# Language-model tower, one core: GpSimd and ScalarE reordered round the low parts of u and xT

## The reference

```python
h = weight[x] * keep_mask[x]                       # 32 x 512 x 256
n = (h - mean(h)) / sqrt(var(h) + 1e-5)
u, res = split(n @ in_proj_w.T, [512])             # 512 columns of u, 256 of res
u = causal_conv4(u, conv_w) + conv_b               # four taps for each channel
delta = softplus(u @ dt_proj_w.T + dt_proj_b)
g = u * sigmoid(delta)
y = scan(state = 0.9 * state + 0.1 * g)            # along the tokens
h = h + y @ out_proj_w.T + res
n2 = layernorm(h)
xd, wd = mx_quantise(n2), mx_quantise(ffn_weight)  # fp6 values, one scale for 32 columns
h = h + xd @ wd.T + ffn_bias
```

## Time and profile before

| quantity | value |
|---|---|
| median of 3 runs | 1024.26 us (1023.52 to 1025.87) |
| the profiled execution | 1026.02 us, of which the trace spans 1024.2 us |
| mean granted clock of TensorE | 0.988 |
| busy: PE, DVE, POOL, ACT | 93%, 81%, 73%, 63% of the span |

### The profile page before, as it was taken

One profiled execution on the slowest core, in us unless ns is written; L12 is line 12 of the kernel. 1 busy time (PEld: TensorE's weight loads), 2 busy tenths in 40 slices (PEclk: granted clock), 3 DMA queues, 4 the chain that ended last, 5 costly groups with the idle time before them and its releaser, 6 DMA issues.

```text
span 1024.2 us, 14964 instructions
## 1 busy us (share of the span) xinstructions
PE 955.7 (93%) x4892; PEld 781.8 (76%) x4892; DVE 829.8 (81%) x1218; ACT 647.2 (63%) x1342; POOL 750.3 (73%) x749
## 2 busy tenths in 40 slices
PE   2689999999999999999999999999999999999996
PEld 1476887777877778787777788777878787878885
DVE  4767988888888888898888888888889878889866
ACT  5755666666667766666676666766666666665541
POOL 6647777777787777878777788777787787776652
PEclk9889999999999999999999999999999999999998
DMA  5213432244433234443223443323444322343101
GB/s 170 69 35 103 123 91 81 88 115 124 124 103 95 77 93 123 123 123 102 77 88 103 123 123 108 94 76 91 123 123 123 102 68 88 112 124 103 62 23 42
DMA packets 73790, 100.81 MB, mean 98 GB/s; under 512 B 12577, under 2 KB 61089, under 8 KB 73761
## 3 DMA queue, kind: packets, MB, share of 16 engines
q1 hardware_dynamic: 67616, 83.59, 25.7%
q0 software_dynamic: 6144, 16.85, 7.2%
HBM read 51.65 MB, written 48.76 MB: 98 GB/s over the span
## 4 chain that ended last, share of the span: by engine, by line
POOL 41%; issue 21%; DVE 20%; PE 9%; ACT 7%; DMA 1%; POOLq 0%; DVEq 0%; ACTq 0%
POOL g_lo L381 16%; POOL rows L366 11%; DVE u L757 10%; POOL xT_lo L430 5%; ACT n L558 4%; DVE h L767 3%; DVE stats L773 3%; POOL rstd L415 3%; POOL h L425 3%; ACT u L515 2%; PE psZ L1074 1%; PE psZ L1068 1%; PE psZ L1067 1%; POOL nmr L419 1%; POOL u_lo L388 1%
## 5 line engine op out<-in xcount | busy, mean ns | idle before, releaser
L757 DVE SCALAR_TENSOR_TENSOR u<-psU,cw,u 128x511 f32<-128x511 f32 x378 | 260.0, 741 | 82.6 <-ACT u L515 80.2
L388 POOL TENSOR_TENSOR u_lo<-u,u_hi 128x512 fp32r<-128x512 f32 x128 | 164.5, 1296 | 83.1 <-ACT u_hi L522 79.0
L1074 PE MATMUL psZ<-u_lo,dt_hi 128*128 128x512 f32 x512 | 208.9, 408 | 12.5 <-POOL u_lo L388 12.5
L381 POOL TENSOR_TENSOR g_lo<-g,g_hi 128x512 fp32r<-128x512 f32 x128 | 199.8, 1580 | 20.6 <-ACT g_hi L533 19.9
L1067 PE MATMUL psZ<-u_hi,dt_hi 128*128 128x512 f32 x512 | 201.4, 393 | 5.7 <-ACT u_hi L522 4.6
L1068 PE MATMUL psZ<-u_hi,dt_lo 128*128 128x512 f32 x512 | 202.2, 395 | 0.0
L522 ACT ACTIVATE u_hi<-u 128x512 fp32r<-128x512 f32 x128 | 81.0, 633 | 138.4 <-DVE u L757 137.7
L366 POOL DMA_INDIRECT rows<-table,ids x128 | 127.1, 993 | 44.9 <-issue 44.1
L1074 PEld LDWEIGHTS psZ<-u_lo,dt_hi 128*128 128x128 f32 x512 | 96.5, 188 | 58.9 <-POOL u_lo L388 40.7
L515 ACT ACTIVATE u<-psU,cb,cw 128x512 f32<-128x512 f32 x126 | 94.3, 772 | 39.7 <-PE psU L1010 39.6
L533 ACT ACTIVATE g_hi<-g 128x512 fp32r<-128x512 f32 x128 | 76.6, 621 | 62.3 <-DVE g L837 62.3
(11 more groups left out here) (120 smaller groups left out, 2215.5 us busy)
## 6 DMA issues: line engine op xcount, KB each, us to landing
turned_n<-nb_blocks SPq DMA_DIRECT2D x31, 512.0 KB
nT<-turned_n SPq DMA_DIRECT2D x124, 128.0 KB
out<-h SPq DMA_DIRECT2D x31, 512.0 KB, 4.6
turned<-xb SPq DMA_DIRECT2D x30, 512.0 KB, 2.6
xT<-turned SPq DMA_DIRECT2D x120, 128.0 KB, 2.9
rows<-table,ids POOLq DMA_INDIRECT x128
dt_stage<-dt_wT SPq DMA_DIRECT2D x1, 1024.0 KB, 5.8
g<-in_wT SPq DMA_DIRECT2D x1, 768.0 KB
```

Of the source, the lines that this page charges most:

```text
L381: pool.tensor_tensor(g_lo[:, m, :], g[:, m, :], f32(g_hi[:, m, :]), ALU.subtract).then_inc(g_lo_ready[m], 1)
L388: pool.tensor_tensor(u_lo[:, m, :], u[:, m, :], f32(u_hi[:, m, :]), ALU.subtract).then_inc(u_lo_ready[m], 1)
L757: dve.scalar_tensor_tensor(u[:, m, back:T], u_psum_tile(st, m)[:, 0:T - back], cw[:, m, TAPS - 1 - back:TAPS - back], u[:, m, back:T], ALU ...
L1074: ins = pe.matmul(psZ[:, m % 2, :], dt_hi[:, k, o], u_lo[:, k, :], start=False, stop=(k == M - 1))
```

## The change

On POOL, g_lo(3) goes ahead of add_bias, mean1 goes behind u_lo(0) and u_lo(1), xT_lo goes ahead of u_lo(2) and u_lo(3), and variance1 with inverse_root1 goes behind them. On ACT, xT_hi goes ahead of the first taps of u(2) and u(3), and the four squares go behind u_hi(2) and u_hi(3). No instruction is added, taken out or changed in size.

```diff
@@ POOL @@
+                if st.back:
+                    split_g(M - 1, s - 1)
                 if st.tail:
                     add_bias()
-                if st.back:
-                    split_g(M - 1, s - 1)
...
-                if st.early:
-                    mean1(2)
                 split_u(0)
                 split_u(1)
                 if st.early:
+                    mean1(2)
+                if st.tail:
+                    split_xT()
+                split_u(2)
+                split_u(3)
+                if st.early:
                     variance1(2)
                     inverse_root1(2)
-                split_u(2)
-                split_u(3)
-                if st.tail:
-                    split_xT()
@@ ACT @@
                 if st.early:
                     mask_rows(2)
-                    square1_rows(2)
+                if st.tail:
+                    split_xT()
                 if not st.first:
                     first_tap(2)
                     first_tap(3)
-                if st.tail:
-                    split_xT()
                 split_u(2)
                 split_u(3)
+                if st.early:
+                    square1_rows(2)
                 if st.early:
                     normalise1(2)
```

## The result

The changed kernel takes **1080.86 us** (median of 3 runs, 1080.83 to 1081.92) against 1024.26 before: a ratio of 1.0553, with a 95% interval of 1.0529 to 1.0577. That is 56.6 us slower. The forecast was slower by 28.2 us, 1053, with a range up to 1069. The direction was right, the size was half of what was measured, and the time lies outside the range.

The account below looks back on a forecast made before the run. PE was taken as the pace until the delayed layer-norm chain replaced it. 0.78 + 0.72 - 0.38 = 1.12 us a step over 27 steps, plus 0.8, less 2.8, gave +28.2: 1053 us, range 1034 to 1069.

Parts of the forecast that it names:

- slack of 0.95 us behind turn_n1: DVE's only slack behind turn_n1, ahead of add_linear; it absorbs 0.95 us of the delay, the rest lengthens the period.
- PE sets the pace: In a full step PE, busy 93% of the span, bounds the kernel; its gaps are at most 2.1 us a step.
- Part 1: POOL's low parts for PE come earlier; alone this would give PE 1.4 us a step back (bounds 1.2 and 2.1).
- each becomes ready before PE asks: g_lo(3), u_lo(0), u_lo(1) and xT_lo, moved earlier on POOL, would no longer keep PE waiting.
- Part 2: ACT's first taps of u(2) and u(3) start 1.60 us earlier; waiting for xT's loads taken as 0, at most 0.3.
- Part 3: Squares and root behind u_hi(3) delay normalise1: turn_n1 1.73 us late, add_linear 0.78 us late, the period longer by 0.78.
- Part 4: POOL's first two g_lo meet DVE's quantisation: round_to_grid's end loses 0.72 us a step, dequantise gives back 0.38.
- rival (b): A worse collision: scale issued over about 1.25 us after the g_lo pair starts; 1.8 us a step, 1071 us; 13%.
- The ends: Steps 30 and 31 have no first layer norm, so PE keeps its prize there: 2.8 us back in all.

Follow-up runs that it names:

- e12: The kernel before plus one tiny POOL operation and a wait for it between the gathers and g_lo(0): 1032.58 us.
- e11: The kernel of e5 plus a tiny POOL operation and a wait for it between the gathers and g_lo(0): 981.05 us.
- e1: The changed kernel, with POOL waiting for DVE's round_to_grid ahead of g_lo(0) in every step from 1 on: 1055.37 us.
- e5: The changed kernel with ACT's squares back behind the first taps, ahead of u_hi(2), and POOL's root ahead of u_lo(2): 1018.29 us.
- e9: The changed kernel plus one tiny POOL operation and a wait for it between the gathers and g_lo(0): 1069.57 us.
- e2: The changed kernel, with POOL waiting ahead of g_lo(0) only until DVE's scale is done: 1068.83 us.
- e8: The changed kernel, with POOL waiting for the end of its own g_lo(0) ahead of g_lo(1): 1065.97 us.
- e10: The kernel of e7 plus a tiny POOL operation and a wait for it between the gathers and g_lo(0): 1060.49 us.
- e7: The kernel before with only the squares moved behind u_hi(3), and epsilon and root behind u_lo(3): 1163.31 us.
- e6: The order of e5, with POOL also waiting for DVE's round_to_grid ahead of g_lo(0): 984.23 us.

## Why the prediction was right and wrong

**What bounds the kernel: right on the slack, too simple on the pace.** The slack of 0.95 us behind turn_n1 decided, as said. But "PE sets the pace" was read from PE's busy share. The chain of the same page gave PE 9% and POOL 41%, and in e12 0.27 us more on DVE came with 0.3 more in the period. This did not make the forecast miss, since the cost was rightly counted from DVE's gapless stretch.

**Part 1: the size right, one statement not.** With the squares out of the way (e11) the period is 28.5 to 28.9 us, so the moves together are worth 1.3 to 1.7 us a step; 1.4 was taken. In e11 PE's loads wait 13.6 us for u_lo instead of 34.0, and the linear layer's wait for xT_lo has left the list. But "each becomes ready before PE asks" did not hold for u_lo in the changed kernel: PE's loads wait 35.6 us for it. There it costs nothing that the rows show, as PE is not in the circle.

**Part 2: right.** The second taps start 1.60 us earlier, as forecast. xT's loads landed in time: ACT never waited for that DMA in the changed kernel's waits.

**Part 3: right.** turn_n1 is 1.80 us late (forecast 1.73) and add_linear 0.84 (0.78). ACT waits 1.72 us for the root. The runs e1 and e5 confirm both sides: 1.02 us a step are left when the meeting is removed, and turn_n1's wait vanishes when the squares go back.

**Part 4: the term that failed.** It read "It loses 0.72 us", and it measured 1.60. The prediction had the scale let in after the first g_lo and round_to_grid delayed by what was left of the pair. What came is that the scale itself was kept out to the end of the pair, 1.80 us instead of 0.18, and round_to_grid ran free behind it, at 1.23. The price came from step 30, where POOL's pair had been waiting 2.71 us for g_hi(0). In the steps that it was used for, the pair follows the gathers without a wait that holds POOL. The prediction took the two for the same meeting because the offset agreed (1.00 forecast, against 0.91). The offset was a poor choice of likeness: e9 shows that the scale gets in at 0.50, if only POOL waits between gathers and pair. A smaller error lies in the same step: the pair was put 0.24 us too early, as the third gather took 1.21 us instead of 0.95.

**The rivals.** What came was close to rival (b), which had 13%: the scale let neither subtraction go first. Its mechanism was right ("round_to_grid followed the pair with scale and reciprocal still to do"), its price, 1.8 us a step, close to the 2.05 measured. Its condition was wrong: it was to decide when the scale comes more than 1.25 us after the pair's start, and it came 0.81 after. So the match in price is partly luck. The range stopped at 1069, short of that rival's own 1071, and the measured 1081 is above both.

**The ends.** Steps 30 and 31 were to give 2.8 us back. The last two periods are 30.98 and 28.20 against 30.34 and 28.57 before, 0.27 us more in sum. Why the prize stays out there is open.

**The Trainium skill.** "SBUF — State Buffer", section "Who interferes with whom", says that a VectorE instruction with two SBUF inputs contends with a GpSimd instruction that reads SBUF, that one in a 2-port mode contends with GpSimd too, that whoever issues first has the shared ports for the whole instruction, and that order of issue decides who blocks. The traces agree on which instructions meet: scale, round_to_grid and dequantise do, the largest value of each block never does (1.20 to 1.22 us in all full steps), and the reciprocal doesn't either (0.35 us beside the running second g_lo of e9). They go further on how long: 7.46 us of dequantise is four whole POOL instructions behind the one under way, so "for the whole instruction" bounds nothing once a row of POOL work follows a gather without a wait that holds POOL.

## What to carry to other kernels

When two engines exclude each other, price the meeting from a place where the *other* engine's instructions stand in the same row, with the same thing ahead of them and the same waits between them. A like offset in time proves nothing. Look for such meetings in the durations of small instructions, not in the waits. If a row of GpSimd work runs behind gathers, a wait in that row lets VectorE in, if GpSimd really has to stand in it. A wait for a tiny operation of its own does that every time, a wait for another engine only when that engine is late. Here the tiny operation was worth 11, 37 and 103 us in three kernels, and cost 6 in a fourth where VectorE was held for one subtraction at most.

Before moving work out of the way of the engine that is the pace, ask who needs its result next. The same four squares cost 0.84 us a step behind u_hi(3). Between the first taps and u_hi(2) they kept turn_n1 waiting in no full step, and with the pause the kernel was 4.4% faster than before.

## What the runs showed of the hardware

- A VectorE instruction that met GpSimd was let in after the g_lo under way when GpSimd had waited between the last gather and that g_lo: 0.83 us for the scale (e9), 1.98 for round_to_grid (e2), 1.87 for dequantise (e12). A wait behind that g_lo did the same: 0.55 for the scale (e8). In e10 dequantise was let in ahead of the first g_lo, 1.22. Without such a wait it was kept out to the end of GpSimd's row: 1.80 us (26 of 27 steps of the changed kernel, two subtractions), 3.25 (its step 25, a gather and two), 3.91 (e5, a gather and two), 7.46 (e7, a gather, three and add_bias).
- A wait that was already met did not count as one: 3.62 us for round_to_grid in step 25 of e2, where it takes 1.97 in the others, and 5.10 for dequantise in step 25 of e6 instead of 1.82.
- VectorE can get in early in a gather, but the time since the gather's start is not all that decides. In the kernel before round_to_grid (509.79, 1.23 us) was issued 0.19 us into the last gather of POOL's timeline:

```profile
509.60 0.95 POOL L366 DMA_INDIRECT rows<-table,ids  x1 [0.30 <-issue]
```

  Issued 0.71 us into one it took 3.91 (e5). The scale, issued 0.31 us into the last gather of step 25, took 0.18 in e2 (847.93) and 3.25 in the changed kernel (858.68). The gathers can be held too: 1.90 us under round_to_grid (e7).
- What the gather itself has to do with it is not shown apart. e9 and e10 show that a wait between gathers and row ends the keeping out; no run has such a row with neither a gather nor a wait ahead of it, and none shows the cause inside the chip.
- In the kernel before, the second g_lo also followed a gather without a wait that held GpSimd, and dequantise got in after the first all the same (1.60 us). There g_lo(0) had itself been held by round_to_grid, which may count as the break in the row. This is an inference; in e7 it was the gather that was held, and that was no break.
